# Even attention steps: side product, routing product and values' product between the second score product and the second maximum product

## The reference

```python
def _L0_attn_ref(x, Wq, Wk, Wv, Wo, bo):            # x: (16, 512, 128), 16 heads of 8
    Q = to_heads(x @ Wq); K = to_heads(x @ Wk); V = to_heads(x @ Wv)
    scores = jnp.einsum('bhqd,bhkd->bhqk', Q, K) * scale
    scores = jnp.where(causal_mask, -1000000.0, scores)
    weights = jax.nn.softmax(scores, axis=-1)
    attn = jnp.einsum('bhqk,bhkd->bhqd', weights, V)
    return attn.reshape(b, s, D_OUT) @ Wo + bo
...
x = _layernorm(x + attention(x))
x = _layernorm(x + mixture_of_experts(x))           # layer norm, top 2 of 8 experts, gelu, 128 -> 512 -> 128
```

## Time and profile before

| | |
|---|---|
| Time, median of 3 runs | 1001.58 us (997.56 to 1003.03) |
| Span of the profiled execution | 999.0 us (its own time is not listed) |
| TensorE, matmuls | 875.7 us busy, 88% |
| VectorE | 740.8 us, 74% |
| ScalarE | 679.0 us, 68% |
| GpSimd | 654.1 us, 65% |
| Mean granted clock of TensorE | 0.975 of full speed |

### The profile page before, as it was taken

How to read it: one execution, slowest core, us unless ns; L and a number is a source line. 1 busy time by engine, 2 the same in 40 slices (tenths; PEclk the granted TensorE clock), 3 DMA queues, 4 the chain that set the end, 5 groups by cost and what they waited for, 6 DMA issues and landing times.

```text
span 999.0 us, 29037 instructions
## 1 busy us (share of the span) xinstructions
PE 875.7 (88%) x9185; PEld 567.4 (57%) x9185; DVE 740.8 (74%) x2029; ACT 679.0 (68%) x1434; POOL 654.1 (65%) x907
## 2 busy tenths in 40 slices
PE   4689898999999999999999989849999999999960
PEld 2334444444444444444544444349999988998860
DVE  1877788888888888888888898935554555458767
ACT  1377687777787777777877877836566655667763
POOL 6243555778778677787777777656767656556652
PEclk9799999999999999999999999979999999999995
DMA  7625534636536345345345332333223323266644
GB/s 198 192 74 158 180 87 153 197 97 191 153 120 207 114 150 178 104 145 167 106 148 172 100 119 67 101 106 89 78 83 89 83 77 88 74 208 189 199 118 147
DMA packets 169379, 132.50 MB, mean 133 GB/s; under 512 B 52938, under 2 KB 155377, under 8 KB 169104
## 3 DMA queue, kind: packets, MB, share of 16 engines
q1 hardware_dynamic: 156880, 112.48, 37.9%
q0 software_dynamic: 8704, 17.06, 5.1%
q10 hardware_dynamic: 3648, 1.12, 0.5%
HBM read 71.55 MB, written 61.15 MB: 133 GB/s over the span
## 4 chain that ended last, share of the span: by engine, by line
PE 51%; POOL 14%; issue 10%; DVE 10%; ACT 7%; DMA 5%; SPq 1%; ACTq 0%; POOLq 0%; DVEq 0%
PE ring L1230 13%; PE ring L1246 12%; PE ps_v L1166 6%; DVE negmax L1277 5%; PE ring L1103 4%; ACT probs L793 4%; POOL probs L661 4%; PE ring L1134 4%; POOL rows_d L703 2%; POOL rs L727 2%; PE ring L1149 2%; PE ps_m L1002 2%; DMA qarea<-mt 2%; DMA qodd<-mt 2%; PE ps_m L996 2%
## 5 line engine op out<-in xcount | busy, mean ns | idle before, releaser
L1277 DVE TENSOR_REDUCE negmax<-ring 128x2 f32<-128x1024 f32 (+3 forms) x512 | 409.3, 814 | 70.3 <-PE ring L1149 66.6
L793 ACT ACTIVATE probs<-ring 128x768 f32<-128x768 f32 (+1 forms) x384 | 335.0, 879 | 113.5 <-PE ring L1103 107.4
L661 POOL TENSOR_SCALAR_AFFINE_SELECT probs<-probs 128x512 f32<-128x512 f32 x256 | 163.2, 640 | 158.3 <-ACT probs L793 156.3
L917 ACT ACTIVATE vpad<-ring,b_s 128x128 f32<-128x128 f32 x576 | 164.9, 370 | 119.9 <-PE ring L1230 119.8
L711 POOL DMA_INDIRECT y_d<-vpad,xs x144 | 146.5, 1018 | 100.3 <-DVE vpad L1588 57.0
L1166 PE MATMUL ps_v<-probs,vpad 128*32 128x512 f32 (+3 forms) x2048 | 180.2, 441 | 8.4 <-POOL probs L661 8.4
L1230 PE MATMUL ring<-vpad,w_t 128*128 128x128 f32 x1152 | 156.0, 279 | 7.3 <-ACT vpad L940 4.6
L1246 PE MATMUL ring<-qarea,vpad 128*128 x1152 | 156.5, 279 | 3.8 <-issue 3.5
L1230 PEld LDWEIGHTS ring<-vpad,w_t 128*128 128x128 f32 x1152 | 141.7, 194 | 9.9 <-ACT vpad L940 6.0
L703 POOL DMA_INDIRECT rows_d<-xn,slot x128 | 128.7, 1005 | 28.4 <-issue 24.7
L1246 PEld LDWEIGHTS ring<-qarea,vpad 128*128 128x128 f32 x1152 | 140.6, 192 | 9.2 <-issue 7.7
(11 more groups left out here) (190 smaller groups left out, 1171.2 us busy)
## 6 DMA issues: line engine op xcount, KB each, us to landing
kside<-qk_d SPq DMA_DIRECT2D x32, 512.0 KB, 7.2
qk_d<-qarea SPq DMA_DIRECT2D x32, 384.0 KB, 2.7
xs<-rows_d SPq DMA_DIRECT2D x144, 66.0 KB
qk_d<-qarea SPq DMA_DIRECT2D x32, 256.0 KB, 2.4
qarea<-qk_d SPq DMA_DIRECT2D x16, 512.0 KB
qodd<-qk_d SPq DMA_DIRECT2D x16, 512.0 KB
probs<-y_d SPq DMA_DIRECT2D x16, 512.0 KB
xin<-L_attn_x SPq DMA_DIRECT2D x16, 256.0 KB, 3.6
```

The source lines that it names most:

```text
L661: pool.affine_select(out=diag, in_=diag, pattern=[[0, 4], [1, P]], compare_op=ALU.is_ge, fill=0.0, base=0, channel_multiplier=-1).then_inc ...
L793: nc.scalar.activation(of_unit(h // 2, part), ring[:, 2 * part % 3, :, (0, P, P)[part]:S], ACT.Exp, scale=SCALE).then_inc(sem("exp_done"), 1)
L917: ins = nc.scalar.activation(ht[:, n % 4, c, :], ps_a[:, n % 4, c * P:(c + 1) * P], ACT.Gelu_apprx_tanh, bias=b1_s[:, bass.ds(e, 1), c:c + ...
L1277: ins = nc.vector.tensor_reduce(negmax[:, n // 6 % 2, qb, s:s + 2], ring[:, (2 * n + 1) % 3, :, c0:c0 + nk], AX.X, ALU.max, negate=True)
```

## The change

In an even step the order on TensorE was s0, m0, side product, s1, wait for m1's bank, router's product, m1, values' product. It becomes s0, m0, s1, side product, router's product, values' product, m1. Where there is a router's product, the wait for m1's bank is made before it, otherwise before m1. Odd steps keep their order: s2, m2, side product, values' product. v moves from step 4 to step 7, and ScalarE's copy of it from the start of step 5 to the end of step 7. ScalarE's copies of xT in step 2 and qT in step 10 move behind the exponentials of s1. The streams of VectorE, GpSimd and SyncE are not changed.

```diff
-        MISC = {1: ("mT", 0, 1), 2: ("xT", 2, 0), 3: ("kT", 2, 0), 4: ("v", 1, 0), 5: ("mT", 0, 2), 6: ("uT", -1, 1),
+        MISC = {1: ("mT", 0, 1), 2: ("xT", 2, 0), 3: ("kT", 2, 0), 5: ("mT", 0, 2), 6: ("uT", -1, 1), 7: ("v", 1, 0),
                 8: ("aT", -1, 0), 9: ("mT", 0, 3), 10: ("qT", 2, 0), 11: ("nT", -2, 0), 12: ("wo", -1, 0),
                 13: ("mT", 1, 0), 14: ("uT", 0, 0)}
...
-                        if h == 5 and u == 0 and nxt.exists(NB):
+                        if h == 7 and u == 2 and nxt.exists(NB):
                             copy_v(act, nxt)
...
+                        if u == (2 if h in (2, 10) else 1):
+                            middle(act, h, i, nxt, prev, rb)
                         if u == 1:
-                            middle(act, h, i, nxt, prev, rb)
...
-            def maxima(b, n, i, h):
+            def claim(b, n, i):
...
-                if n % 3 == 1:
-                    spare(i, b, h)
+
+            def maxima(b, n):
...
                     scores(i, h // 2, 2 if h % 2 else 0)
-                    maxima(mb, mu + (2 if h % 2 else 0), i, h)
+                    claim(mb, mu + (2 if h % 2 else 0), i)
+                    maxima(mb, mu + (2 if h % 2 else 0))
+                    if h % 2 == 0:
+                        scores(i, h // 2, 1)
                     if h in MISC:
                         misc(i, *MISC[h])
...
-                    if h % 2 == 0:
-                        scores(i, h // 2, 1)
-                        maxima(mb, mu + 1, i, h)
+                    if h in (LG_STEP, RK_STEP):
+                        claim(mb, mu + 1, i)
+                        spare(i, mb, h)
                     if h % 4:
                         vb, vg = (i, h // 4 - 1) if h >= 4 else (i.plus(-1), 3)
                         values(vb, vg, ((0,), (1,), (3, 2))[h % 4 - 1])
+                    if h % 2 == 0:
+                        if h not in (LG_STEP, RK_STEP):
+                            claim(mb, mu + 1, i)
+                        maxima(mb, mu + 1)
```

More of the change, by code:

```diff
@@ L1126, in maxima @@
                     need(pe, sem("max_taken"), AUNITS, b, n - 2)
-                if n % 3 == 1:
-                    spare(i, b, h)
+            def maxima(b, n):
+                if not b.exists(NB):
+                    return
                 blocks = (((3, S, 0),), ((2, 3 * P, 0),), ((0, 2 * P, 0), (1, 2 * P, 2 * P)))[n % 3]
```

## The result

The changed kernel takes 1030.35 us, median of 4 runs (1025.78 to 1033.33). The kernel before took 1002.31 beside it (4 runs, 997.56 to 1003.33). The ratio is 1.0286, with a 95% interval from 1.0255 to 1.0317: slower by 2.9%. The forecast was 1040, in a range of 1021 to 1053. The profiled execution took 1025.78 us and spans 1024.0, which is 25.0 more than the span before.

What follows compares the result with a forecast made beforehand. TensorE was taken to bound the kernel, VectorE close behind. Terms of 3.4 us per full block gave 37 for blocks 3 to 13, plus 6.5 for other blocks, less 5 for uneven waits: +38.5, median 1040, range 1021 to 1053.

Steps and rivals of the forecast that it cites:

- rival 2: Only v's wait in step 7 costs, nT's in step 11 doesn't: 14 us under the forecast, 1026; chance 0.15.
- v enters step 7: In steps 6 and 7 v waits for VectorE's divide to read uT, behind a later m1: 2.65 us more per block.
- nT in step 11: nT waits for VectorE's reader of qT, behind the maximum of a later m1: 1.2 us more per block.
- Steps 14 to 1: s1 of step 14 waits for step 13's last maximum, +0.4 us; step 1's wait for GpSimd gives 0.4 back.
- Steps 8 and 9: VectorE is fresh after the wait for v: 0.2 us less per block.
- v leaves step 4: Taking v's 1.1 us out of step 4 returns only 0.2 us, as m2 still waits for ScalarE.
- Step 2: s1 waits 0.2 to 0.3 us for step 1's last maximum, against 0.1 saved: +0.1 us per block.
- Step 12: One entry less from 64-row into full-height products: 0.1 us less per block.
- Blocks 0, 1, 2 and 14: Block 0 has no wait; blocks 1, 2 and 14 cost 1.8, 2.7 and 2.0: 6.5 us together.
- Uneven waits: In blocks 3 to 13 the new idle time takes in waits of uneven blocks: 5 us less over the run.
- 1 (faster): Fewer entries and ready exponentials win, freeing of ps_m is no limit: 10 us less, 991; chance 0.05.
- Rival 3: Collisions with GpSimd's L742 hold VectorE in step 6 too: 1.0 us more in 13 blocks, 1053; chance 0.13.

Runs made afterwards that it cites:

- The first experiment: Changed kernel with v and ScalarE's copy of it back in steps 4 and 5, new order kept: 1003.86 us, ratio 1.0036 to the kernel before.

## Why the prediction was right, and where its terms were off

The forecast was that v and nT wait for VectorE's readers behind a late m1, and that the entries won give back less. That held in both places; the error is in sizes, and in one wait that did not come (step 2). The sum for a full block was 3.4, measured 2.65. With 1030.35 the time lies nearer to rival 2's 1026 than to the forecast of 1040, though rival 2's reason is refuted: the terms that were off add up to 10.9 us (below), where that rival took 14 off.

- **v enters step 7**: 2.65 forecast, 2.57 measured. m1 at 2.6 forecast, 2.50 measured; end of the divide 5.2 and 5.13; v at 5.3 and 5.19; idle 1.7 and 1.63. The experiments confirm the cause (divide first: -1.70) and the lower bound (m1 not late: 0.98 of idle time, 0.8 forecast).
- **nT in step 11**: 1.2 forecast, 1.12 measured. s1 came 0.92 after s0 (with 0.20 of waiting) where I took 1.0, so m1 came at 3.03 and not 3.1. Reader first: -1.12.
- **Steps 14 to 1**: +0.4 and -0.4 forecast, +0.41 and -0.47 measured. s1 of step 14 waits 0.52; the values' product of step 1 no longer waits for GpSimd (8.4 to 0.8 us over the run), where s2 of step 1 now waits 0.49.
- **Steps 8 and 9**: -0.2 forecast, -0.21 measured. The first experiment shows what this rests on: without the wait for v, s1 of step 8 waits 0.93.
- **v leaves step 4**: -0.2 forecast, -0.28 measured, -0.27 with the move alone. But in the new order v in step 4 is free (4.49 against 4.48). What the new order gives in step 4 and what v's leaving gives are the same quarter of a microsecond, and only one of the two can be had. The forecast had that number and not this reading of it.
- **Step 2**: +0.1 forecast, -0.25 measured. This is the term that failed most. I let s1 wait 0.2 to 0.3 us for the last maximum of step 1. It does not wait: the maximum is done at 486.05, and s1 has its turn only at 486.33, behind the wait in s2 of step 1. The first row is VectorE's, the second TensorE's:

```profile
485.64 0.41 DVE L1286 TENSOR_REDUCE negmax<-ring 128x2 f32<-128x256 f32 x1
...
486.33 0.33 PE L1104 MATMUL ring<-qodd,kside 64*128 64x384 bf16 x2
```

- **Step 12**: -0.1 forecast, -0.26 measured. Here as in step 2 nothing waits, before or after, and one entry fewer came with a quarter of a microsecond. With 0.10 us per entry I had 0.7 in a block; the products take 0.96 less, 0.14 per entry. So the saving was larger than I took it, and the row's price is not all of it. The rule of the Trainium skill, TensorEngine Tiling (Array Packing), Key Properties, that a change of tiling mode drains the array, allowed for more than the row's price. The trace fits it in direction, but no run here tells a longer drain from a better overlap of weight loads. One step of that working was wrong: changes between 128-wide and 32-wide products do not just remain, the change adds them in steps 2, 6, 7, 10 and 14, where a side or router's product now stands directly ahead of the values' product.
- **Blocks 0, 1, 2 and 14**: +6.5 forecast, +2.9 measured. Block 0 gets 1.0 us shorter (I had 0), block 1 1.5 longer (1.8), block 2 1.35 (2.7), block 14 1.1 (2.0). A good part is waits that I had counted from block 3 on alone: ahead of s0 of step 4 TensorE waited for the copied maxima 0.90 us in block 1 (at 85.26) and 0.67 in block 2 (at 123.71) before, and 0.38 and not at all after. In block 0 the wait of 0.76 us before v is gone with v's place.
- **Uneven waits**: -5 forecast. In the changed kernel blocks 4 to 13 are even, and blocks 3 to 13 grow by 24.7 us, where 11 x 2.65 would be 29.2: -4.5. Right.

Together: the forecast was 7.8 us too long in the full blocks (37 - 29.2), 3.6 in the others, and 0.5 too short in the uneven waits, which makes 10.9. From the first s0 of block 0 to that of block 15 the kernel is 27.6 us longer, where 38.5 was forecast. The span grows by 25.0, as the time behind the last exponential is 3.6 us shorter in this execution. The medians are 28.0 apart, where 38.4 was forecast.

The rivals: 1 (faster) and 4 (no change) fell with the wait of 1.63 us. Rival 2 fell with the run that has qT's reader first. Rival 3, that GpSimd holds VectorE in step 6 too, did not happen: GpSimd's L742 ran from 497.58 to 498.84, over both readers of rk (L1375, L1377), and they took 0.19 and 0.17 us, as in every block (durations below: least, median, most). VectorE keeps its written order: it sat idle for 0.64 us before L1375 with uT ready. This is what the Trainium skill, TensorE: Matmul & The Clock Gate, architectural detail, says of its queue, and the trace agrees.

```profile
L1375 DVE TENSOR_TENSOR rt<-ring,used x13: 190/192/192, 170.3 to 658.5; 128x32 f32<-128x32 f32 x13
...
L1377 DVE TENSOR_TENSOR used<-ring,used x13: 166/166/167, 170.5 to 658.7; 128x8 f32<-128x8 f32 x13
```

The stated signs came as well: period 40.99 (41 to 42), 1.63 before v (1.7), 1.05 before nT (1), 0.52 before s1 in step 14 (0.3 to 0.7). Before s1 in step 10 it is 0.20, a little less than said, and the wait in step 2 did not come.

## What to carry to other kernels

Where several products share one buffer, moving a product means moving the reader of the product before it as well: look up where that reader stands in its own engine's order, and what it stands behind. A reader that stands behind a later maximum turned a saving of about 1 us a block into a loss of 2.65, and the same order with two readers moved, and v left where it was covered, is 1.4% faster than the kernel before (two more moves: 1.6 to 2% on three chips). And a product that fills another's wait is free where it is: the same 1.1 us of v cost nothing in step 4, and 0.6 to 0.9 in step 7 even with its reader first.

## What the runs showed of the hardware

- A small VectorE operation whose operands all lie in SBUF, L1373, seems to be held while a GpSimd operation runs: it takes between 0.15 and 1.39 us over 14 blocks, and 0.46 in block 11, where it ended with GpSimd's mask (497.61). Its like in the kernel before took 0.89 in the earlier trace rows. The operations of similar size behind it that also read a ring bank of PSUM (L1375, L1377) never moved by more than 2 ns. That the operand in PSUM makes the difference is my reading; no run measured it by itself.
- The same program takes 5% more on some chips: the kernel before took 999.37 us on one and 1046.68 to 1050.73 on three others, each over 11 to 19 runs. Of this some 6 to 9 us can be the stall in step 4 (0.9 us in seven to ten blocks). Most of it lies behind the blocks, where the experts' tiles run: from the start of the last exponential to the end of the span the profiles have 347 to 353 us in the six runs without the stall, and 394 to 398 in the seven with it. Why that part is longer I did not take apart. A ratio is only good on one chip.
